# A graph network kernel whose edge sort becomes a streamed counting sort, with the weights loaded beside the scatter

## What is computed

```python
s = s @ W_nl0
v = jnp.einsum('nmi,mk->nki', v, W_nl1)
w = jax.nn.relu(edge_feature @ W_fc1) @ W_fc2
xs = s[dst]
xv = v[dst]
...
agg = jax.ops.segment_sum(tp, src, num_segments=N) / DENOM
out_s = agg_s @ W_out_s + skip_s
```

## Time and profile before

| | us |
|---|---|
| median of 3 runs | 11428.95 |
| lowest, highest | 11417.05, 11443.12 |
| span of the profiled execution | 10605.0 |

### The profile page before, as it was taken

How to read it: one execution, slowest core, us unless ns; L and a number is a source line. 1 busy time by engine, 2 the same in 40 slices (tenths; PEclk the granted TensorE clock), 3 DMA queues, 4 the chain that set the end, 5 groups by cost and what they waited for, 6 DMA issues and landing times. The chain is left out here.

```text
span 10605.0 us, 244487 instructions
## 1 busy us (share of the span) xinstructions
PE 8843.7 (83%) x46500; PEld 6209.7 (59%) x46501; DVE 8615.3 (81%) x31135; ACT 6948.2 (66%) x26255; POOL 6456.4 (61%) x9505
## 2 busy tenths in 40 slices
PE   3571049999999999999998989887899998988987
PEld 1250048888888888888885444446444446444445
DVE  7850049999999999999997999994677776999995
ACT  0020048888888888888885666663688885777774
POOL 0477777777777777777652555550466661555551
PEclk9965579999999999999998999996899998999996
DMA  7433322122222212222112444442233343444443
GB/s 299 41 81 76 70 48 36 36 36 37 36 36 36 36 36 36 36 36 36 26 20 70 92 92 92 92 91 42 52 67 67 67 65 67 93 93 93 92 92 58
DMA packets 1798441, 691.91 MB, mean 65 GB/s; under 512 B 1586190, under 2 KB 1677258, under 8 KB 1798346
## 3 DMA queue, kind: packets, MB, share of 16 engines
q0 software_dynamic: 219136, 411.56, 16.0%
q1 hardware_dynamic: 1572154, 275.26, 15.5%
q10 hardware_dynamic: 7056, 4.02, 0.1%
HBM read 514.24 MB, written 171.77 MB: 65 GB/s over the span
## 5 line engine op out<-in xcount | busy, mean ns | idle before, releaser
L914 POOL DMA_INDIRECT shared<-table,rec x2640 | 2551.0, 966 | 1969.1 <-issue 820.9
L997 PE MATMUL bank<-tp,oh 128*128 128x480 f32 (+1 forms) x2640 | 1281.1, 567 | 198.6 <-DVE tp L1074 184.9
L948 ACT ACTIVATE tp<-tp,rec 128x64 f32<-128x64 f32 x3960 | 1017.4, 335 | 335.4 <-DVE tp L1045 322.6
L989 PE MATMUL bank<-w_fc,hT 128*128 128x448 f32 x2640 | 1216.4, 543 | 3.1 <-ACT hT L932 3.1
L782 POOL DMA_INDIRECT rec_dst<-ACC x784 | 812.4, 1036 | 530.6 <-issue 498.5
L1597 POOL DMA_INDIRECT gat<-table,rec x880 | 890.6, 1012 | 219.7 <-issue 197.0
L1633 ACT ACTIVATE shared<-bank 128x512 f32<-128x512 f32 x1760 | 942.8, 585 | 122.4 <-PE bank L1708 119.5
L1584 POOL DMA_INDIRECT rec_src<-ACC x784 | 842.1, 1074 | 207.4 <-issue 185.5
L1708 PE MATMUL bank<-ident,tp 128*128 128x128 f32 x7040 | 932.9, 276 | 3.3 <-ACT tp L813 2.0
L983 PEld LDWEIGHTS bank<-efT,w_fc 128*128 128x128 f32 (+1 forms) x2640 | 457.9, 187 | 713.9 <-ACT efT L927 627.5
L1708 PEld LDWEIGHTS bank<-ident,tp 128*128 128x128 f32 x7040 | 830.4, 147 | 3.9 <-ACT tp L813 2.3
(11 more groups left out here) (265 smaller groups left out, 24040.8 us busy)
## 6 DMA issues: line engine op xcount, KB each, us to landing
shared<-table,rec POOLq DMA_INDIRECT x2640
rec_dst<-tp SPq DMA_DIRECT2D x44, 900.0 KB, 23.6
ACC<-in_attrs SPq DMA_DIRECT2D x56, 623.0 KB
rec_src<-tp SPq DMA_DIRECT2D x44, 730.0 KB, 19.8
efr<-rec_src SPq DMA_DIRECT2D x440, 64.0 KB
efr<-rec_dst SPq DMA_DIRECT2D x440, 64.0 KB
ACC<-in_attrs SPq DMA_DIRECT2D x196, 130.0 KB
rec<-rec_dst SPq DMA_DIRECT2D x1320, 10.0 KB
```

What stands on the lines that cost most here:

```text
L914: nc.gpsimd.indirect_dma_start(out=gatx[:, u, g, 0:L.row], out_offset=None, in_=tables[L.n][:, :], in_offset=IOff(ap=rec[:, u, g, L.idx:L. ...
L948: done = nc.scalar.activation(t[:, g, lo:lo + 64], t[:, g, 0:64], ACT.Copy, scale=rec[:, u, g, L.y + k:L.y + k + 1])
L989: nc.tensor.matmul(pW[u % 2][:, 0:448], hT[:, u % 2, :], fc2[:, :], start=True, stop=True)\
L997: done = nc.tensor.matmul(pS[u][:, 0:TW], oh[:, u, g, :], products[u][:, g, 64:64 + TW], start=g == 0, stop=g == G - 1)
```

## The change

Blocks 1 and 2 are gone; all their work stands in block 3.

- SP loads the keys first, then the attributes of the first two chunks, fills `rec_dst`, loads `X`, `a_rows` and the axes, and only then the first two chunks' places. In the loop it waits for a chunk's places to be ranked (`ranked`) and for the chunk before to be placed.
- The weights are loaded from ACT's queue, after POOL has cleared their tiles. ACT then waits until `rec_dst` is filled, and fills `rec_src`.
- POOL waits until `rec_dst` is filled, then scatters as before. The padding is marked by the host's key (block 49), not by POOL.
- DVE and PE sort in another way. A chunk is now CC = 7 columns by WB = 50 blocks, 350 elements; there are 112 chunks. *Counting*: DVE compares the chunk's keys with all block numbers (`one_hot_blocks`), PE adds the columns' counts with a product with ones. *Offsets*: 15 short steps. *Ranking*: for each chunk PE adds up three products in one bank (offsets, edges ahead in the same column, edges of the chunks before), DVE picks each edge's own number (`picked`), sums it (`summed`), writes it as an integer (`placed_at`), and makes the next chunk's comparison (`hot`) and running sum (`passed_by`). An edge's place in its block is another than before.
- The weights are prepared (`weights_ready`, `weights_tensor`) after both sorts, ahead of the first node pass.

```diff
+        WB, CC = NB + 1, 7
+        NQ = T // (4 * CC)
+        LB = CC * WB
...
+        def one_hot_blocks(i, u, s):
+            return nc.vector.tensor_tensor(
+                eqb[:, u], blkf[s][:, columns(i, u)].unsqueeze(2).to_broadcast([P, CC, WB]),
+                bidx.unsqueeze(1).to_broadcast([P, CC, WB]), ALU.is_equal)
...
+        def count_vector(ve, s):
+
+            with ve.Fori(0, NQ) as i:
+                for u in range(4):
+                    ve.wait_ge(count_added[s].h, count_added[s].free(i, u, 4))
+                    one_hot_blocks(i, u, s).then_inc(count_hot[s].h, 1)
...
+            def hot(i, u):
+                ve.wait_ge(rank_before[s].h, rank_before[s].free(i, u, 3))
+                one_hot_blocks(i, u, s).then_inc(rank_hot[s].h, 1)
+
+            def passed_by(i, u):
+                ve.wait_ge(rank_hot[s].h, rank_hot[s].done(i, u))
+                ve.wait_ge(rank_passed[s].h, rank_passed[s].free(i, u, 1))
+                nc.vector.tensor_tensor(passed[:, (u + 1) % 4], passed[:, u], eqb[:, u], ALU.add)\
+                    .then_inc(rank_passed[s].h, 1)
+
+            def picked(i, u):
+                ve.wait_ge(rank_before[s].h, rank_before[s].done(i, u))
+                nc.vector.tensor_tensor(prod[:, u % 2], eqb[:, u],
+                                        pRank[u % 2].rearrange("p (c b) -> p c b", c=CC), ALU.mult).then_inc(rank_read[s].h, 1)
+
+            def summed(i, u):
+                ve.wait_ge(rank_read[s].h, rank_read[s].done(i, u))
+                nc.vector.reduce_sum(posr[:, u % 2, :], prod[:, u % 2], AX.X).then_inc(rank_summed[s].h, 1)
+
+            def placed_at(i, u):
+                ve.wait_ge(rank_summed[s].h, rank_summed[s].done(i, u))
+                nc.vector.tensor_copy(pos_of[s][:, columns(i, u)], posr[:, u % 2, :]).then_inc(ranked[s].h, 1)
...
+            with pe.Fori(0, NQ) as i:
+                for u in range(4):
+                    r = pRank[u % 2]
+                    pe.wait_ge(rank_read[s].h, rank_read[s].free(i, u, 2))
+                    nc.tensor.matmul(r, ident[:, :], off.rearrange("p c b -> p (c b)"), start=True, stop=False)
+                    pe.wait_ge(rank_hot[s].h, rank_hot[s].done(i, u))
+                    nc.tensor.matmul(r, tril[:, :], flat_hot(u), start=False, stop=False)
+                    pe.wait_ge(rank_passed[s].h, rank_passed[s].free(i, u, 1))
+                    nc.tensor.matmul(r, ones[:, :], passed[:, u].rearrange("p c b -> p (c b)"),
+                                     start=False, stop=True).then_inc(rank_before[s].h, 1)
...
             @block.vector
             def _(ve):
+                nc.vector.memset(zeros_t, 0.0).then_inc(zero_tile, 1)
+                nc.vector.memset(zrow, 0.0).then_inc(const_ready, 1)
+                nc.vector.memset(ones[:, :], 1.0).then_inc(const_ready, 1)
+                split_keys(ve, 0)
+                ve.wait_ge(ramp_done, 7)
+                count_vector(ve, 0)
+                offsets(ve, 0)
+                rank_vector(ve, 0)
                 pair_table(ve, 0)
-                bucket_vector(ve, 1)
+                split_keys(ve, 1)
+                count_vector(ve, 1)
+                offsets(ve, 1)
+                rank_vector(ve, 1)
                 pair_table(ve, 1)
+                weights_ready(ve)
...
             @block.scalar
             def _(ac):
+                ac.wait_ge(setup_zero, 1)
+                for dst, src in loads:
+                    ac.dma_start(dst, src, allow_slow_non_contiguous=dst.shape[-1] == 1).then_inc(weights_in, 16)
+                ac.wait_ge(zero_tile, 1)
+                ac.wait_ge(fill_done[0], 16 * NFILL)
+                v = rec_src.rearrange("(k p g) r -> k p (g r)", p=P, g=ZP * G)
+                for k in range(NFILL):
+                    ac.dma_start(v[k], zeros_t[:, 0:ZP * G * RS]).then_inc(fill_done[1], 16)
```

More of the change, by code:

```diff
@@ L523, in bucket_tensor @@
         def bucket_tensor(pe, s):
-            def add(rows, **kw):
-                for n, (lo, hi) in enumerate(TH):
-                    last = nc.tensor.matmul(BK[2 * s + n][:, 0:hi - lo], ident[:, :], rows[:, lo:hi], **kw)
-                return last
-            add(zrow, start=True, stop=False)
-            with pe.Fori(0, HB) as i:
-                for u in range(2):
-                    pe.wait_ge(picked[s].h, picked[s].done(i, u))
-                    add(tmb[:, u, :], start=False, stop=False).then_inc(added[s].h, 1)
@@ new lines, in flat_hot @@
+            def flat_hot(u):
+                return eqb[:, u].rearrange("p c b -> p (c b)")
+            if s:
+                pe.wait_ge(off_step, OFF_STEPS)
+            nc.tensor.matmul(pCount, ones[:, :], zrow, start=True, stop=False)
+            with pe.Fori(0, NQ) as i:
+                for u in range(4):
+                    pe.wait_ge(count_hot[s].h, count_hot[s].done(i, u))
+                    nc.tensor.matmul(pCount, ones[:, :], flat_hot(u), start=False, stop=False)\
+                        .then_inc(count_added[s].h, 1)
@@ new lines, in bucket_tensor @@
+            nc.tensor.matmul(pCount, ones[:, :], zrow, start=False, stop=True).then_inc(off_step, 1)
+            pe.wait_ge(off_step, OFF_STEPS * (s + 1))
+            with pe.Fori(0, NQ) as i:
+                for u in range(4):
+                    r = pRank[u % 2]
[6 more added lines that the diff above has]
+                                     start=False, stop=True).then_inc(rank_before[s].h, 1)
```

380 lines of the change are left out of this document (174 added, 206 removed).

## The result

The changed kernel is slower: 11696.27 us (median of 4 runs, 11692.69 to 11751.67) against 11423.0 us for the kernel before beside it (4 runs), a ratio of 1.0247 with a 95% interval of 1.0228 to 1.0266. The forecast was 11272 us, in a range of 11200 to 11380.

A forecast was written before the change was run, and what follows sets the result against it. The prediction took the record scatter to bound the stage before the edge loops: start 240 us, 403 issues at 1.35 us, 381 at 1.287 us, end 1274 instead of 1431 us, so 11428.95 - 157 = 11272 us; range 11200 to 11380 us.

The forecast's parts named there:

- I carry this difference unchanged: Whole kernel: the median lies 823.95 us above the profiled span, and this was added unchanged to the forecast span of 10448 us.
- the scatter sets the end of this stage: Stage before the edge loops: only the record scatter, last issued at 1429.88 us, decides when the first edge loop starts.
- The first node pass, 153 us in the earlier trace, then ends at 937 us: After both sorts: DVE is at 784 us, the pass takes 153 us and ends at 937 us, hidden beside the scatter.
- the start of the scatter: POOL's first scatter issue: 240 us, the middle between bounds of 195 and 275 us, against 342.59 us before.
- rival 1: Loads wait for the rec_src fill: scatter starts at 275 us, ends at 1308 us, kernel 11306 us; chance 0.22.
- a ranking chunk: New sort's ranking loop: picking, comparison, two products, drain and semaphores take 2.42 us a chunk, 271 us in all.
- the granted clock of 1.00 undisturbed: PE in the new sort loops: granted clock stays 1.00, so a product of 350 columns takes 0.59 us.
- issues beside the new loops aren't longer: POOL's scatter beside the sort: 0.5 us DVE operations show no port-lock price; an issue alone is 0.97 us.
- the sum: Scatter start, lower bound: rec_dst filled at 115 us, plus 10 for X and 68 for the axes, 193 us.
- The pace: Scatter issue spacing: 1.35 us beside the sort until 784 us (403 issues), then 1.287 us alone (381 issues).
- Rival 5: Scatter beside the sort: POOL waits at DVE's operation boundaries, 2.2 us an issue, end 1475 us, kernel 11473 us; chance 0.06.
- Rival 3: Sort becomes the bound: PE at lower clock, 1.17 us a product, first pass ends 1333 us, kernel 11331 us; chance 0.06.

The follow-up runs named there:

- the second execution of the kernel before: The kernel before the change, unedited, profiled once more: 11395.78 us (one run), with a span of 11394.1 us.
- the kernel with 448 columns: Changed kernel with one POOL memset of 448 columns, and a wait, after each indirect DMA of the scatter: 11438.79 us.
- the kernel with two products: Changed kernel with the offsets put into the running sum's first row, so TensorE does two products a ranking chunk, not three: 11843.94 us.
- the first page: Profile of the unedited kernel before that the prediction was made from: span 10605 us.
- three memsets: Changed kernel with three POOL memsets of 448 columns, each with a wait, after each indirect DMA of the scatter: 12590.7 us.
- 128 columns: Changed kernel with one POOL memset of 128 columns, and a wait, after each indirect DMA of the scatter: 11341.2 us.
- the bare wait: Changed kernel with no memset, only a semaphore increment by POOL and a wait for it after each indirect DMA of the scatter: 11185.24 us.
- these gathers 448 columns: Kernel before the change with one POOL memset of 448 columns, and a wait, after each gather of layers 1 to 3: 11010.06 us, 0.9689.
- 128 did nothing: Changed kernel with bf16 sort rows and a 128-column POOL memset after each scatter DMA and each gather of layers 1 to 3: 11175.98 us.

## Why the prediction was wrong

- *The base.* The step that failed first: "I carry this difference unchanged". The page showed an undisturbed execution, and the 824 us lay inside the span of the usual ones. A page that is 7% below all times of its kernel shows an execution unlike the ones that are timed, not the same one with something around it. In the second execution of the kernel before, block 3 was ended by the first node pass (over at about 1580 us), not by the scatter (1495 us), so "the scatter sets the end of this stage" did not hold there.
- *The second step that failed:* "The first node pass, 153 us in the earlier trace rows, then ends at 937 us", and with it all rows of the sort beside the scatter. Every one of PE's instructions was priced as if the scatter weren't there; in the chunks that are held up it costs 1.3 to 1.4 us on average. The changed kernel has 12 of them for 7 columns, 1344 a pass of ranking. The bucket sort's first loop kept its pace beside the scatter; that may be due to its long DVE operations, or to the issues beside it, which come mostly 1.67 us apart, a spacing at which the new ranking isn't delayed either. No run separates the two. The first node pass ended at about 1835 us, not 937.
- *Right:* the start of the scatter (forecast 240 us, measured 250.6, so rival 1 was out), a ranking chunk (2.42 us, measured 2.49), the granted clock of 1.00 undisturbed, and that issues beside the new loops aren't longer (972 ns in the median, 0.97 us alone). The start was in part luck: the sum had no term for `a_rows`, whose issue (25 KB) held SP for 67.29 us behind X, so that the axes were issued only at 158.94 us; they landed 89.1 us later. On the length of an issue the Trainium skill, "SBUF — State Buffer", section "SBUF: two separate sides", spoke against this change with its lock of the shared port; in the kernel with 448 columns the ranking ran at 2.49 us beside issues of 972 ns in the median, so for operations of 0.5 us neither side paid here. Whether the issue of an indirect DMA is an operation that the rule speaks of, no run shows.
- *The pace:* 1.35 us was forecast beside the sort and 1.287 alone; on average it was 1105 / 783 = 1.41 us. The issue is as short as assumed and mostly follows after 1.28 us, but 15 times, mostly where the chunk changes, the next comes only after 3 to 6 us. That SP's small instructions are late too (below) would explain it, but was not tested.
- *Rival 5* had the right sign by a mechanism that didn't act: POOL's issues kept 1.28 us and 972 ns, they did not wait for DVE's boundaries. *Rival 3*, PE at the lower clock, was seen in the kernel with two products.
- *What stays open:* by what path POOL's issues delay TensorE. The records place the delay between a product and its semaphore but, since a product's end is modelled, can't tell whether the products run late or their semaphores do. Why the first page's execution escaped it is open too: its issues were 1.28 us apart as well, and PE did 490 matmul instructions in 153 us beside them. Its gathers come in pairs and not in bursts, but that may be the consequence. And whether the wait or the small instructions beside it help was not taken apart.
- *A rival that no run tests:* that recording the execution has a part in the delay. The delay goes with lost records: a DMA here adds 16 to its semaphore, and from 600 to 900 us the traces hold 99% of these updates on the first page and with three memsets, 64% with 448 columns, 22% with 128 columns or with the bare wait, and 11 to 12% in the changed kernel and in the second execution of the kernel before; the whole trace of that kernel has 209666 semaphore updates on the first page and 105210 in the second execution. Perhaps the updates themselves crowd a path that PE's semaphores need, perhaps their records do; but the first page, with nearly every update recorded, is the execution without the delay. No run compares an execution that is recorded with one that isn't.

## What to carry to other kernels

Compare the span of a page with the measured times before reading anything else; if they differ by per cents, the page isn't the execution that is measured. Work beside a loop of indirect DMAs may have to be priced by its count of TensorE instructions, not by their durations alone; look in the trace for VectorE waiting long after the product is over. Then try a wait behind each indirect DMA, which takes three lines. How long a pause pays has to be measured at each place: in this scatter a bare wait or 128 columns won, while 448 columns took all of the delay away but made the scatter so long that nothing was left of it against the kernel before; in these gathers 448 columns won and 128 did nothing.

## Hardware behaviour that was not expected

- Beside indirect DMAs issued back to back by POOL, 1.28 us apart with no wait between, 12 TensorE instructions took 16.7 us instead of 2.49, or 1.4 us each on average; on the first page, at the same spacing, nothing was delayed. A wait after each, at the same spacing: 3.9 us. A spacing of 1.62 us: 2.49 us.
- It doesn't need the rows' bytes to be moved (16.9 us with all but one place dropped, though the packets remain), and the DMA engines' load isn't it: at 100 to 200 us, with a DMA share of 1.04, the ranking ran at full speed.
- Other engines' small instructions lengthen as well. SP's issue of a load takes 0.70 or 1.40 us in the changed kernel and 0.39 us in the one with three memsets:

```profile
601.31 0.70 SPq L698 DMA_DIRECT2D ACC<-in_attrs  x1
619.09 1.40 SPq L698 DMA_DIRECT2D ACC<-in_attrs  x1
```

```profile
608.08 0.39 SPq L700 DMA_DIRECT2D ACC<-in_attrs  x1
```

- The same kernel has an execution with a span of 10605 us and others of about 11400 us. POOL's gathers last as long in both (966 and 968 ns on average) and DVE's operations nearly so (L1085: 611 and 614 ns); the waits are longer.
